# Softmax denominators as 128 queries by 8 in an attention block: one small inversion, turned together with the next head's maxima

## The chip, the cores and the metric

The kernel runs on one core of a Trainium2 chip. It is one launch, written out instruction by instruction for each engine: TensorE multiplies matrices, VectorE, ScalarE and GpSimd work on elements, and SyncE issues the transfers. The engines run side by side and are held together by semaphores alone. The metric is the device time of the launch in microseconds (us).

## What is computed

A transformer block on x of shape 2 x 1024 x 128: a modulated attention layer with 16 query heads of 64 (4 key heads), rotary positions and an ALiBi bias, then two layers of local attention and gated MLP. The change touches the first attention alone, whose core is

```
attn = einsum('bhqd,bhkd->bhqk', q, k) / sqrt(64)
attn = attn + slopes[None, :, None, None] * rel[None, None, :, :]
attn = softmax(attn, axis=-1)
out  = einsum('bhqk,bhkd->bhqd', attn, v)
```

Two batches of 16 heads make 32 heads of 1024 queries by 1024 keys. Softmax needs of each query its maximum over the keys, ahead of the exponential, and the sum of the exponentials, its denominator, by which the output is divided.

## The kernel before

The heads run one after another. Each is cut into eight steps k of 128. Two different tilings are in use. The *maxima* of head i+2 are taken with 128 queries on the partitions and 1024 keys along the row (`max_step`: a product on TensorE into banks 4 and 5, L836, then one VectorE instruction that adds the ALiBi row and keeps the negated maximum, L765). They end as a tile M of 128 queries by 8 steps. The *scores* proper have 128 keys on the partitions and 1024 queries along the row (`qk_step`, L862, into banks 0 and 1 or 2 and 3, by turns; the exponential on ScalarE, L738; the product with the values, `pv_step`, L872, into bank 6 or 7). So the maxima are needed as a row over the queries: TensorE turns M (`turn_m`, L842), ScalarE copies it out (`take_m`, L721), and SyncE moves it into QM (`load_m`, L639), from where it enters the score product of the next head.

The denominators of head i-1 are made in head i. GpSimd and VectorE add up the eight exponentials into `sum_p` (128 keys by 1024 queries). TensorE sums over the partitions with a stationary block of ones, 32 wide, four times 256 queries, so that the result stands on four groups of partitions as 256 queries a row (`denominators`, L881, into bank 0). ScalarE copies it out (`take_denominators`, L715), VectorE inverts it in two halves of 128 columns, each spread over all 128 partitions (`invert`, L782). SyncE stores the 1024 inverses to memory and loads them back, broadcast over the partitions (`spread_inverse`, L645 and L649), and VectorE multiplies the finished output by them (`divide`, L790), which frees the bank of head i-1 for head i+1.

The order is written out by hand. TensorE runs, for each pair of steps k, k+1: two score steps, the maxima of step k of head i+2, two value steps (k-1 and k), and the maxima of step k+1. Behind the value steps of the second pair stand the small products: the denominators of head i-1 and the turn of head i+1. The score step k = 4 waits for the two copies on ScalarE, since bank 0 holds the denominators and bank 1 the turned maxima. The first value step of head i waits until head i-2 is divided. VectorE runs the maxima k = 0 to 7, with a sum ahead of k = 0, the inversions behind k = 2 and 3, another sum behind k = 5 and the two divisions behind k = 6. SyncE runs in a head: the loads for later heads, `load_m`, then `spread_inverse`.

Of the kernel before, what the change touches and what calls it, by code (L numbers as in the profile page):

```python
# [13 lines left out]
P = 128  # L14
B, N, D = 2, 1024, 128
TB = N // P
# [75 lines left out]
def adaln_block(nc, x, wq, wk, wv, wo, f_wqkv, f_qs, f_ks, f_wo, f_lg, f_lb, f_w1, f_b1, f_w2, f_b2,  # L92
# [7 lines left out]
    with ExitStack() as whole:  # L100
# [478 lines left out]
        DQ = N // 4  # L579
        with ExitStack() as ph:  # L580
# [3 lines left out]
            M = sb("M", [P, 2, TB])  # L584
            mrow = sb("mrow", [TB, 2, P], F32R)
# [4 lines left out]
            den_sb = XF[:, TB + 2:TB + 2 + DQ // P, :].rearrange("p t d -> p (t d)")  # L590
            den_inv = XF[:, TB:TB + DQ // P, :].rearrange("p t d -> p (t d)")
# [10 lines left out]
            m_turned = sem("m_turned")  # L602
            mrow_done = sem("mrow_done")
# [6 lines left out]
            den_taken = sem("den_taken")  # L610
# [14 lines left out]
            def m_bank(i):  # L625
                return 1 if i > 0 else 7
# [4 lines left out]
            with nc.Block() as block:  # L631
                @block.sync
                def _(sp):
                    def load_m(i, s):

                        sp.wait_ge(qm_filled, 3)
                        need(sp, mrow_done, i + 1)
                        for ch in range(2):
                            sp.dma_start(QM[HD * ch:HD * ch + 1, s, :].bitcast(F32).rearrange("p (t c) -> p t c", c=P),  # L639
                                         mrow[TB // 2 * ch:TB // 2 * (ch + 1), s, :].bitcast(F32)).then_inc(ld_m[s], 16)  # L640

                    def spread_inverse(i, s):

                        need(sp, inv_done, 2 * (i + 1))
                        sp.dma_start(inv_d[s].rearrange("(c n) -> c n", n=DQ), den_inv[0:P:32, :]).then_inc(inv_out, 16)  # L645
# [56 lines left out]
                def _(act):  # L702
# [9 lines left out]
                    def take_denominators(i):  # L712
                        need(act, den_mm, i + 1)
                        need(act, inv_done, 2 * i)
                        act.activation(den_sb[:, :], banks(den_bank(i))[:, 0:DQ], ACT.Copy)\  # L715
                            .then_inc(den_taken, 1)

                    def take_m(i, s):
                        need(act, m_turned, i + 1)
                        need(act, ld_m[s], 32 * (i // 2))  # L720
                        act.activation(mrow[:, s, :], banks(m_bank(i))[0:TB, 0:P], ACT.Copy).then_inc(mrow_done, 1)  # L721

                    def head(i):
                        for k in range(TB):
                            if k == 4 and i > 0:
                                take_denominators(i - 1)
                            if k == 4 and i + 1 < HEADS:
                                take_m(i + 1, (i + 1) % 2)
# [21 lines left out]
                    take_m(0, 0)  # L750
# [809 lines left out]
```

## Time and profile before

| | |
|---|---|
| time, median of 3 runs | 1317.8 us (1313.16 to 1318.82) |
| the profiled execution | 1316.46 us, of which the span of the trace is 1314.7 |
| busy share of the span | TensorE 85%, VectorE 80%, GpSimd 65%, ScalarE 56% |
| exponentials, L738 | 256 of 1112 ns, 274.8 us |
| maxima on VectorE, L765 | 256 of 1209 ns, 309.4 us |
| inversions, L782 | 64 of 948 ns, 60.4 us, and 64.1 us of idle time ahead of them |
| copy of the denominators, L715 | 32 of 383 ns, 12.3 us |

In the rows, PE is TensorE's products and PEld its loads of the stationary operand, DVE is VectorE, ACT ScalarE, POOL GpSimd, and SPq the issuing of transfers by SyncE. A product of 32-bit numbers appears as two records, each with its own load: the four products of the denominators are eight. Matrix products overlap, so that starts are more telling than durations. "M" and "mrow" are the maxima, "XF" is the memory in which denominators and inverses lie, "xpos_sb" that of the sums.

### The profile page before, as it was taken

How to read it: one execution, taken by the hardware profiler on the slowest of the kernel's cores; microseconds unless marked ns; L12 is line 12 of the kernel's file. 1: busy time of each engine (PE TensorE's matmuls, PEld its weight loads, DVE VectorE, ACT ScalarE, POOL GpSimd, SP SyncE). 2: the span in 40 equal slices, each digit the busy share in tenths (PEclk: the TensorE clock that was granted, in tenths of full speed). 3: DMA queues.
4: the chain of work that ended last, by engine and by line, in shares of the span. 5: the costliest groups of instructions: out<-in, count | busy, mean ns of one | idle time of the engine just before them, and what ended most of it. 6: DMA issues, size and time to landing. Idle time of an engine off the chain costs nothing. (4 is left out here: it accounts for less than half of the span.)

```text
span 1314.7 us, 23737 instructions
## 1 busy us (share of the span) xinstructions
PE 1115.1 (85%) x8256; PEld 692.6 (53%) x8256; DVE 1049.2 (80%) x2026; ACT 735.6 (56%) x1512; POOL 849.0 (65%) x488
## 2 busy tenths in 40 slices
PE   5776579999999999999999999467777896778788
PEld 3554535544455454555445548234555684455578
DVE  6898577777777777777777746599999589999957
ACT  3666625555555555555555551257676755777664
POOL 4556216566566666656656664698789249999916
PEclk9888769999999999999999999789898997999899
DMA  7567932142413314241331001000111100111111
GB/s 230 136 173 198 283 80 57 42 97 65 105 42 86 76 42 97 65 105 38 83 83 52 23 17 56 34 17 19 27 28 28 31 3 8 27 28 29 30 31 33
DMA packets 95237, 88.91 MB, mean 68 GB/s; under 512 B 22884, under 2 KB 74768, under 8 KB 95120
## 3 DMA queue, kind: packets, MB, share of 16 engines
q1 hardware_dynamic: 95120, 87.41, 26.2%
q8 instruction: 66, 1.08, 0.3%
q14 instruction: 51, 0.42, 0.1%
HBM read 53.57 MB, written 24.25 MB: 59 GB/s over the span
## 5 line engine op out<-in xcount | busy, mean ns | idle before, releaser
L738 ACT ACTIVATE E<-psum,keybias_sb 128x1024 f32<-128x1024 f32 x256 | 274.8, 1112 | 249.1 <-PE psum L862 235.9
L765 DVE CUSTOM_DVE_ANT_0 junk<-psum,alibi 128x1024 bf16<-128x1024 f32 x256 | 309.4, 1209 | 93.0 <-PE psum L836 80.2
L684 POOL TENSOR_TENSOR xpos_sb<-xpos_sb,E 128x1024 f32<-128x1024 f32 x96 | 231.2, 2408 | 130.7 <-ACT E L738 126.2
L872 PE MATMUL psum<-E,V 128*64 128x512 f32 x1024 | 248.0, 605 | 0.0
L836 PE MATMUL psum<-KH,QH 64*128 64x512 f32 x512 | 124.7, 481 | 20.9 <-DVE M L765 16.7
L688 POOL TENSOR_TENSOR xpos_sb<-xpos_sb 128x1024 f32<-128x1024 f32 x32 | 76.1, 2377 | 90.7 <-DVE xpos_sb L775 90.7
L1195 ACT ACTIVATE E_att<-S_att,nmax_att 128x128 f32<-128x128 f32 x256 | 99.0, 389 | 43.7 <-DVE nmax_att L1229 43.6
L1142 POOL TENSOR_TENSOR rinv_att<-ss_up_att,minus_half 128x16 f32<-128x16 f32 x32 | 120.8, 3775 | 2.7
L872 PEld LDWEIGHTS psum<-E,V 128*64 128x64 f32 x1024 | 62.1, 136 | 112.7 <-issue 105.7
L836 PEld LDWEIGHTS psum<-KH,QH 64*128 64x128 f32 x512 | 50.6, 191 | 124.1 <-DVE M L765 92.6
L782 DVE RECIPROCAL XF<-XF 128x128 f32<-128x128 f32 x64 | 60.4, 948 | 64.1 <-ACT XF L715 64.1
L862 PE MATMUL psum<-QH,KH 64*128 64x512 f32 x512 | 106.4, 406 | 3.4 <-ACT XF L715 1.0
L862 PE MATMUL psum<-QL,KH 64*128 64x512 f32 x512 | 103.4, 392 | 0.0
L862 PE MATMUL psum<-QH,KL 64*128 64x512 f32 x512 | 103.1, 391 | 0.0
L862 PE MATMUL psum<-QM,one_rows 64*128 64x512 f32 x512 | 103.0, 390 | 0.0
L1132 POOL TENSOR_TENSOR t_att<-raw_att,xpos_sb 128x1024 f32<-128x1024 f32 x32 | 100.5, 3142 | 0.0
L1323 PE MATMUL psum<-kT_att,qT_att 64*64 64x128 f32 x1024 | 42.4, 310 | 66.3 <-DVE nmax_att L1229 66.1
L684 POOL TENSOR_TENSOR xpos_sb<-E 128x1024 f32<-128x1024 f32 x32 | 76.4, 2388 | 30.0 <-ACT E L738 24.8
L1248 DVE TENSOR_TENSOR qk_att<-qk_att,rinv_att 128x1024 f32<-128x1024 f32 x32 | 90.3, 2823 | 5.8 <-POOL rinv_att L1142 4.7
L1323 PEld LDWEIGHTS psum<-kT_att,qT_att 64*64 64x64 f32 x1024 | 33.9, 152 | 88.6 <-issue 88.0
L1127 POOL TENSOR_TENSOR sq_att<-raw_att 128x1024 f32<-128x1024 f32 x32 | 66.6, 2083 | 14.1 <-ACT raw_att L1202 14.1
L1313 PE MATMUL psum<-fw_qkv,hT_att 128*128 128x512 f32 x128 | 66.1, 642 | 2.1 <-ACT raw_att L1202 2.1
(145 smaller groups left out, 2399.9 us busy)
## 6 DMA issues: line engine op xcount, KB each, us to landing
qa_scratch<-tT SPq DMA_DIRECT2D x32, 512.0 KB, 4.1
QH<-qa_scratch SPq DMA_DIRECT2D x64, 256.0 KB, 4.2
QL<-qa_scratch SPq DMA_DIRECT2D x64, 128.0 KB, 4.2
XF<-inverse_scratch SPq DMA_DIRECT2D x64, 128.0 KB, 2.9
vp_att<-v_att SPq DMA_DIRECT2D x64, 128.0 KB, 2.3
k_scratch<-tT SPq DMA_DIRECT2D x16, 256.0 KB, 4.6
KH<-k_scratch SPq DMA_DIRECT2D x16, 256.0 KB, 3.9
KL<-k_scratch SPq DMA_DIRECT2D x16, 256.0 KB, 5.1
```

Source lines behind the costliest of these rows:

```text
L684: pool.tensor_tensor(sum_p[:, s, :], first, E[:, k % 4, :], ALU.add)\
L688: pool.tensor_tensor(sum_p[:, s, :], sum_p[:, s, :], sum_d[:, s, :], ALU.add)\
L738: act.activation(E[:, k % 4, :], scores(k % 2), ACT.Exp, bias=kb).then_inc(exp_done, 1)
L765: dve.tensor_tensor_reduce(junk[:, :], banks(max_bank(i, k), 2), alibi[:, s, :], -1.0, BIG, ALU.add, ALU.min, M[:, s, k:k + 1]).then_inc(m ...
L836: last = pe.matmul(banks(max_bank(i, k) + ch), QH[rows, s, k * P:(k + 1) * P], KH[rows, g, ch * 512:(ch + 1) * 512], start=True, stop=True)
L862: last = pe.matmul(scores(k % 2)[:, ch * 512:(ch + 1) * 512], key[rows], query[rows, a:a + 512], start=(n == 0), stop=(n == len(terms) - 1))
L872: last = pe.matmul(banks(6 + i % 2)[HD * ch:HD * ch + HD, :], V[:, g, k, :], E[:, k % 4, ch * 512:(ch + 1) * 512], start=(k == 0), stop=(k ...
L1132: pool.tensor_tensor(t2[:, s].rearrange("p (q h) d -> p q h d", q=2), raw[:, s].rearrange("p (q h) d -> p q h d", q=2), sin, ALU.mult)\
L1142: pool.tensor_tensor(rinv[:, s, :], ss_up[:, s, :], minus_half[:, 0:NH], ALU.pow)\
L1195: act.activation(E[:, s, h, :], S[:, s, h, :], ACT.Exp, bias=nmax[:, s, h:h + 1], scale=-1.0, accum_out=den[:, s, h:h + 1]).then_inc(exp_d ...
L1248: dve.tensor_tensor(qk[:, s], qk[:, s], rinv[:, s, :][:, :, None].to_broadcast([P, NH, HD]), ALU.mult).then_inc(qk_done, 1)
L1323: last = pe.matmul(banks(5 + h % 2)[WIN * w:WIN * w + WIN, (h // 2) * P:(h // 2 + 1) * P], qT[a:a + HD, s, h // 2, WIN * w:WIN * w + WIN], ...
```

## The change

The denominators are made with the sum stationary and one column of ones moving: eight products, each of which gives 128 queries on the partitions in one column, 128 by 8 in all. VectorE inverts them straight from bank 0 in one instruction, into a tile `stats` beside the maxima. Where the maxima of head i+1 were turned alone (8 columns), one turn now takes them and the inverses of head i-1 (16 columns); one copy on ScalarE takes both out, and SyncE stores the inverses from eight rows of 128. The copy of the denominators and its semaphore are gone.

The order changes with it. The denominators stay where they were on TensorE. The turn moves from behind them to behind the value steps of the third pair (k = 4); the copy from ScalarE's step 4 to step 6; the inversion stands behind the maxima of k = 3, and the divisions move from behind the maxima of k = 6 to behind those of k = 7. The score step k = 4 waits for the inversion, and k = 6 for the copy. At the end of the stage the last turn stands behind the fourth tile of the output projection.

```diff
 def spread_inverse(i, s):
-    need(sp, inv_done, 2 * (i + 1))
-    sp.dma_start(inv_d[s].rearrange("(c n) -> c n", n=DQ), den_inv[0:P:32, :]).then_inc(inv_out, 16)
+    need(sp, turned_done, i + 3)
+    sp.dma_start(inv_d[s].rearrange("(t c) -> t c", c=P), turned[TB:2 * TB, s, :]).then_inc(inv_out, 16)
...
-def take_denominators(i):
-    need(act, den_mm, i + 1)
-    need(act, inv_done, 2 * i)
-    act.activation(den_sb[:, :], banks(den_bank(i))[:, 0:DQ], ACT.Copy).then_inc(den_taken, 1)
-def take_m(i, s):
-    need(act, m_turned, i + 1)
-    need(act, ld_m[s], 32 * (i // 2))
-    act.activation(mrow[:, s, :], banks(m_bank(i))[0:TB, 0:P], ACT.Copy).then_inc(mrow_done, 1)
+def take_turned(i, s):
+    need(act, stats_turned, i + 1)
+    need(act, ld_m[s], 32 * min(i // 2, HEADS // 2))
+    need(act, inv_out, 16 * (i - 3))
+    rows = TB if i < 2 else 2 * TB
+    act.activation(turned[0:rows, s, :], banks(turn_bank(i))[0:rows, 0:P], ACT.Copy).then_inc(turned_done, 1)
...
-            if k == 4 and i > 0:
-                take_denominators(i - 1)
-            if k == 4 and i + 1 < HEADS:
-                take_m(i + 1, (i + 1) % 2)
+            if k == 6:
+                take_turned(i + 1, (i + 1) % 2)
...
-def invert(i, half):
-    need(dve, den_taken, i + 1)
-    need(dve, inv_out, 16 * i)
-    part = slice(half * DQ // 2, (half + 1) * DQ // 2)
-    dve.reciprocal(den_inv[:, part], den_sb[:, part]).then_inc(inv_done, 1)
+def invert(i, s):
+    need(dve, den_mm, i + 1)
+    need(dve, stats_turned, i + 1)
+    dve.reciprocal(stats[:, s, 1, :], banks(den_bank(i))[:, 0:TB]).then_inc(inv_done, 1)
...
-            if k in (2, 3) and i > 0:
-                invert(i - 1, k - 2)
+            if k == 3 and i > 0:
+                invert(i - 1, (i - 1) % 2)
...
-            if k == 6 and i > 0:
+            if k == 7 and i > 0:
                 for ch in range(2):
                     divide(i - 1, ch)
...
 def denominators(i, s):
-    for c in range(4):
-        last = pe.matmul(banks(den_bank(i))[32 * c:32 * c + 32, 0:DQ], ones[:, :],
-                         sum_p[:, s, c * DQ:(c + 1) * DQ], start=True, stop=True)
+    for c in range(TB):
+        last = pe.matmul(banks(den_bank(i))[:, c:c + 1], sum_p[:, s, c * P:(c + 1) * P], ones[:, 0:1],
+                         start=True, stop=True)
...
 def qk_step(i, k):
         if k == 4:
-            need(pe, den_taken, i)
-            need(pe, mrow_done, min(i + 2, HEADS))
+            need(pe, inv_done, i)
+        if k == 6:
+            need(pe, turned_done, i + 2)
```

TensorE in the middle of a head, before: behind two value steps (E, V) the denominators (`ones_m`), the turn of the maxima M, the maxima of step 3, and the score step 4 with its waits.

```order
L872 MATMUL psum<-E,V 64x512
L881 MATMUL psum<-xpos_sb,ones_m 32x256 [waits sum_p_done,filled]
L881 MATMUL psum<-xpos_sb,ones_m 32x256 x3
L842 MATMUL psum<-ident,M 8x128 [waits max_done]
L836 MATMUL psum<-KH,QH 128x512 [waits max_done]
L836 MATMUL psum<-KH,QH 128x512
L862 MATMUL psum<-QH,KH 128x512 [waits exp_done,mrow_done,den_taken]
```

The same place now, and the end of the next round, where the turn of `stats` stands.

```order
L873 MATMUL psum<-ones_m,xpos_sb 128x1 [waits sum_p_done,filled]
L873 MATMUL psum<-ones_m,xpos_sb 128x1 x7
L824 MATMUL psum<-KH,QH 128x512 [waits max_done]
L824 MATMUL psum<-KH,QH 128x512
L854 MATMUL psum<-QH,KH 128x512 [waits exp_done,inv_done]
...
L864 MATMUL psum<-E,V 64x512
L832 MATMUL psum<-ident,stats 16x128 [waits inv_done,max_done]
L824 MATMUL psum<-KH,QH 128x512 [waits max_done]
L824 MATMUL psum<-KH,QH 128x512
L854 MATMUL psum<-QH,KH 128x512 [waits exp_done,turned_done]
```

The turn has left its place between denominators and maxima and comes a round later; the score step 4 waits for VectorE instead of ScalarE, and the score step 6 has a new wait.

VectorE, before, from the maxima of step 5 on (`junk,M`) to the first maxima of the next head.

```order
L775 TENSOR_TENSOR xpos_sb<-E 128x1024 [waits sum_p_done,sum_d_done,exp_done]
L765 ISA junk,M<-psum,alibi 128x1024 [waits max_done,max_mm]
L765 ISA M 128x1
L790 TENSOR_TENSOR OT<-psum,XF 64x512 [waits pv_done,inv_in] x2
L765 ISA junk,M<-psum,alibi 128x1024 [waits max_done,max_mm]
L765 ISA M 128x1
L775 TENSOR_TENSOR xpos_sb<-xpos_sb,E 128x1024 [waits sum_d_done,exp_done]
L765 ISA junk,M<-psum,alibi 128x1024 [waits m_turned,max_done,alibi_done,max_mm]
```

The same stretch now.

```order
L766 TENSOR_TENSOR xpos_sb<-E 128x1024 [waits sum_p_done,sum_d_done,exp_done]
L756 ISA junk,stats<-psum,alibi 128x1024 [waits max_done,max_mm]
L756 ISA stats 128x1
L756 ISA junk,stats<-psum,alibi 128x1024 [waits max_done,max_mm]
L756 ISA stats 128x1
L779 TENSOR_TENSOR OT<-psum,XF 64x512 [waits pv_done,inv_in] x2
L766 TENSOR_TENSOR xpos_sb<-xpos_sb,E 128x1024 [waits sum_d_done,exp_done]
L756 ISA junk,stats<-psum,alibi 128x1024 [waits stats_turned,max_done,alibi_done,max_mm]
```

The two divisions (OT), which wait for the loaded inverses, have moved behind the last maxima; behind them now stand the sum and the first maxima of the next head.

## Rows read from the trace of the kernel before

**Rows 1.** The page's first line: the span.

```profile
span 1314.7 us, 23737 instructions
```

**Rows 2.** Busy time by stretch: length, busy us (records) by engine, clock, transfers' share, GB/s.

```profile
240.00:780.00 540.00, 528.71 (x3398) 270.42 (x3394) 411.71 (x607) 283.79 (x308) 337.63 (x142) 1.00 0.27 68
```

**Rows 3.** Timeline, TensorE's loads: start, us, instruction; denominators of first and 29th head.

```profile
212.08 0.16 PEld L881 LDWEIGHTS psum<-xpos_sb,ones_m 128*32 128x32 f32 x8 [0.81 <-issue]
...
750.80 0.16 PEld L881 LDWEIGHTS psum<-xpos_sb,ones_m 128*32 128x32 f32 x8 [0.81 <-issue]
```

**Rows 4.** Timeline, TensorE's loads in one regular head.

```profile
289.11 0.16 PEld L881 LDWEIGHTS psum<-xpos_sb,ones_m 128*32 128x32 f32 x8 [0.81 <-issue]
...
289.68 0.08 PEld L842 LDWEIGHTS psum<-ident,M 128*8 128x8 f32 x1 [0.41 <-issue]
...
289.88 0.19 PEld L836 LDWEIGHTS psum<-KH,QH 64*128 64x128 f32 x2
...
290.42 0.21 PEld L862 LDWEIGHTS psum<-QH,KH 64*128 64x128 f32 x2 [0.35 <-ACT XF L715]
...
294.62 0.19 PEld L836 LDWEIGHTS psum<-KH,QH 64*128 64x128 f32 x2 [0.81 <-DVE M L765]
...
298.98 0.19 PEld L836 LDWEIGHTS psum<-KH,QH 64*128 64x128 f32 x2 [0.81 <-DVE M L765]
...
308.06 0.16 PEld L881 LDWEIGHTS psum<-xpos_sb,ones_m 128*32 128x32 f32 x8 [0.81 <-issue]
```

**Rows 5.** Timeline of the same head, ScalarE and VectorE.

```profile
290.10 0.25 ACT L721 ACTIVATE mrow<-psum 8x128 fp32r<-8x128 f32 x1
...
293.67 1.15 ACT L708 ACTIVATE alibi<-far_sb,slope_sb 128x1024 f32<-128x1024 f32 x1
...
295.16 1.23 DVE L765 CUSTOM_DVE_ANT_0 junk<-psum,alibi 128x1024 bf16<-128x1024 f32 x1 [0.94 <-PE psum L836]
...
301.17 1.22 DVE L775 TENSOR_TENSOR xpos_sb<-xpos_sb,E 128x1024 f32<-128x1024 f32 x1
302.31 1.22 DVE L765 CUSTOM_DVE_ANT_0 junk<-psum,alibi 128x1024 bf16<-128x1024 f32 x1
```

**Rows 6.** Timeline, transfers and divisions: the regular head, then a fourth one.

```profile
290.42 1.29 SPq L639 DMA_DIRECT2D QM<-mrow  x2
293.17 0.51 SPq L645 DMA_DIRECT2D inverse_scratch<-XF  x1
294.83 1.14 SPq L649 DMA_DIRECT2D XF<-inverse_scratch  x2
...
298.59 1.40 DVE L790 TENSOR_TENSOR OT<-psum,XF 64x512 f32<-64x512 f32 x2
...
504.64 0.52 SPq L645 DMA_DIRECT2D inverse_scratch<-XF  x1
507.60 1.14 SPq L649 DMA_DIRECT2D XF<-inverse_scratch  x2
...
511.58 1.41 DVE L790 TENSOR_TENSOR OT<-psum,XF 64x512 f32<-64x512 f32 x2 [1.43 <-DMA XF<-inverse_scratch]
```

**Rows 7.** Timeline, three runs of loads elsewhere in the kernel.

```profile
4.69 2.63 PEld L461 LDWEIGHTS psum<-silu,wmod_sb 128*128 128x128 f32 x12 [4.69 <-DMA wmod_sb<-in_L_wmod_dram]
...
795.58 3.65 PEld L543 LDWEIGHTS psum<-wo_sb,OT 128*128 128x128 f32 x32 [0.81 <-issue]
...
891.18 0.89 PEld L1323 LDWEIGHTS psum<-kT_att,qT_att 64*64 64x64 f32 x32 [2.78 <-issue]
```

**Rows 8.** Instructions by line: busy us, mean ns, idle before; a small reciprocal.

```profile
L1267 DVE RECIPROCAL den_inv_att<-den_att 128x8 f32<-128x8 f32 x32 | 6.1, 192 | 8.9 <-ACT E_att L1195 8.9
```

**Rows 9.** Busy time by stretch, columns as in rows 2.

```profile
881.00:884.30 3.30, 0.88 (x3) 0.06 (x1) 3.27 (x2) 2.01 (x4) 2.85 (x2) 1.00 0.05 12
884.40:887.60 3.20, 2.61 (x10) 2.32 (x11) 3.17 (x5) 1.45 (x3) 1.37 (x2) 0.50 0.29 64
...
512.60:514.40 1.80, 0.22 (x2) 0.03 (x1) 1.77 (x4) 1.46 (x2) 0.00 (x0) 1.00 0.66 150
```

## What the change will do to the time

> **What bounds the kernel now.** I read the profile in this order: the page for the span, the busy time by stretch, the timeline of one head of the attention stage, engine by engine, and then single rows as prices. The profiled execution has a span of 1314.7 us [rows 1] and a device time of 1316.46 us, 1.76 us more; the sum below is made against 1316.5. The median of the three timed runs, 1317.8, is 1.3 above it. The change lies wholly in the attention stage of 32 heads. There TensorE is busy 528.7 of 540 us at the high clock, VectorE 411.7, ScalarE 283.8, GpSimd 337.6 [rows 2]. So TensorE's own order is the bound, and a microsecond taken from VectorE or ScalarE is worth nothing unless TensorE waits for it.
>
> The denominators of one head are issued once per head, so their rows are a ruler: from the first at 212.08 to the one at 750.80 lie 28 heads, 19.24 us each [rows 3]. A regular head runs from 289.11 to 308.06, 18.95 us [rows 4]. It has four rounds of the same work (odd maxima, two score steps, even maxima, two value steps) with a small insert. The unhindered round is 294.62 to 298.98, 4.36 us. The first, 289.88 to 294.62, takes 4.74, since the fifth score step waits for ScalarE's copies until 290.42; from that step to the round's end are 4.20. Denominators and turn together take 0.77 (289.11 to 289.88). The last two rounds take 9.08, which is 0.36 over twice 4.36. So four rounds are 17.44, the insert 0.77, and only about 0.75 is waiting. The reciprocals that the change shrinks cost almost nothing there.
>
> **Denominators.** Before: four products, in the trace eight records of 32 stationary and 256 moving columns, 0.57 us (289.11 to 289.68 [rows 4]). After: eight products with 128 stationary columns and one moving, so 16 loads of 128 columns with nothing long to hide behind. The nearest row is the output projection, 32 pairs of load and product of 128 columns in 3.65 us, 0.114 each [rows 7], which gives 16 x 0.114 = 1.83. Lower bound: 32 pairs of 64x64 in 0.89 us, 0.028 each, 0.45 in all; upper: 12 pairs of 128 stationary and 2 moving columns at the kernel's start, 2.63 us, 0.219 each, 3.5 in all [rows 7]. I take 1.83, since the loads there have the same width and clock, and call it D.
> The Trainium skill ("TensorE: Matmul & The Clock Gate", LDWEIGHTS) says that a load costs by its columns, whatever the rows; the row agrees. The same page's table of issue gaps (Back-to-back issue gap) gives about 60 cycles at 2.4 GHz for any product of up to 64 moving columns; by that, 16 would be 0.4 us and the sum some 40 us lower.
>
> **The wait at the fifth score step.** It now waits for the inversion, because the denominators lie in its bank. On VectorE the inversion stands behind the maxima of step 3, and those stand behind their product on TensorE, issued after the denominators. Walk, from the start of the denominators: product at D, VectorE starts 0.54 later (294.62 to 295.16), the maxima take 1.23, an inversion of 128x8 takes 0.19 [rows 4, 5, 8], and the signal 0.07 (ScalarE done at 290.35, TensorE on at 290.42 [rows 4, 5]). The step starts at D + 2.03. Before it started 0.54 behind that product. The queue behind it is the whole of TensorE: score steps, maxima, value steps.
>
> **The turn, moved behind the value steps.** It starts at D + 2.03 + 4.20 = D + 6.23. Before, its copy on ScalarE was done 0.67 after it (289.68 to 290.35) and the next consumer ran at 0.74. ScalarE is free by then: its two exponentials and the ALiBi row end at 294.82, 4.4 behind the fifth score step [rows 5], here at D + 6.4. So the seventh score step, which waits for the copy, starts at D + 6.97, and the third round begins at D + 6.97 + 4.20 = D + 11.17. ScalarE's other copy goes; it was hidden behind TensorE's maxima.
>
> **The inverse's way through memory.** Here is the main loss. SyncE first issues the two transfers of the next maxima, 1.29, at D + 6.97, then the store at D + 8.3. From store to first load: 1.66 (293.17 to 294.83); from first load to the division that waited for it: 3.98 (507.60 to 511.58) [rows 6]. The divisions can start at D + 13.9; the two take 1.41, done at D + 15.35. Before, the store was issued 4.06 behind the denominators (293.17), and the division found its data there with no wait at 298.59 in a regular head [rows 6].
> The divisions now stand behind the last maxima, which frees the first maxima of the next head from them; but the first value step of the next head needs their bank. It would run at D + 11.17 + 4.36 - 0.93 = D + 14.6 and runs at D + 15.4: 0.8 waited. More weighs what is queued behind them on VectorE: the sum (1.14) and the maxima of step 0 (1.22) [rows 5], and TensorE's maxima of step 1 need that bank pair: 15.35 + 1.14 + 1.22 + 0.07 = D + 17.8, where the round would have ended at D + 15.5. The fourth round adds 4.36: the next denominators start at D + 22.16. They close the loop, since it leads from denominators to denominators: its length is the new period, 1.83 + 22.16 = 24.0 us.
>
> **Cover.** VectorE loses two long reciprocals a head and gains one of 0.19; worth nothing, as VectorE is idle a quarter of the stage [rows 2]. GpSimd's last sum starts once VectorE's sum is done (D + 16.5), and the next denominators, which need it, come 5.6 later. The maxima's transfers land some 2 us behind D + 8.3, needed at D + 11.3: hidden, with 1 us to spare. One thing is better: in each fourth head the store took 2.96 until the load (504.64 to 507.60 [rows 6]), beside the key and value loads; the later store is clear of those. The average of 19.24 contains that loss, so it is counted.
>
> **Sum.** 28 heads x (24.0 - 19.24) = 133. The two heads without maxima lose less, about 2.5 each as an estimate from the same walk, since nothing stands ahead of the inversion and behind the division: 5. At the end the last turn waits for two projection tiles (3.65, [rows 7]) instead of ScalarE: 1 to 2. Together 139.5: 1456 us with the clock untouched.
>
> **The clock.** In [rows 9] the granted clock is 1.00, that is 2.4 GHz, in 881.0 to 884.3, where TensorE was busy 0.88 of 3.3 us, and 0.50, or 1.2 GHz, in the 3.2 us behind. In 512.6 to 514.4, with 0.22 busy of 1.8 between full stretches, it was not lost. The new head has, from the denominators to the fifth score step, D + 2.03 = 3.9 us with 0.34 us of streaming products in it; whether 16 loads with one column each keep the clock up, no row shows. A stretch at the low level as long as that row's costs half of it, 1.65 us, and here wholly on the loop. I take it for a third of the heads, 9 x 1.65 = 14: **forecast 1470 us**. If the one-column products count as work, it is 1456; if not, two thirds of the heads or more, 1487.
> The Trainium skill (same page, Part 1: The HAM clock gate) says that activity releases the throttle and idling brings it back; by that the second case is open, and its price is the one just worked out from rows.
>
> **Rivals.** (1) The loop as walked, clock kept or lost in part: 1445 to 1495, chance 0.70. (2) The clock is lost in most heads and loads run at 0.219: D = 3.5 adds 1.7 x 28 = 47 to 1475: 1495 to 1530, chance 0.13. (3) One-column products are cheap, D = 0.45: 1.38 x 28 = 39 off, 1417 with the clock kept and 1431 with it lost as above: 1410 to 1435, chance 0.13. (4) Not slower: the loop through the inverse does not close, because the inverse lands before the next head's first value step and the inversion slips in before the fifth score step; then TensorE's own work stands, 17.44 + 0.20 + D. That is 19.5 with D = 1.83, 7 us slower in all; with D below 1.6 it is equal, with D = 0.45, 18.1, 32 us faster, 1284. For it speaks that TensorE is 98% busy; against it that both waits are in the order and the walk has them 1.5 and 3.1 us late. That the change would not do what it says is out: the order shows the small inversion and the joint turn where the text puts them. Chance 0.04.
>
> **How the numbers follow.** The range, 1425 to 1525, reaches from part of (3) to nearly all of (2) and leaves some 0.15 out. About 0.5% is what a measurement of this kernel can tell from no change. Faster by more 0.02, within 0.01, slower 0.97.
>
> **What would show each step.** The period of the denominators near 24 us instead of 19.2; their duration near 1.8; a TensorE wait of about 1.5 us for the inversion ahead of the fifth score step; the store about D + 8.3 behind them; waits for the division ahead of a value step and for the maxima behind it; granted clock below 1.00 in some heads. The prediction is wrong if the fifth step does not wait, or if the divisions start earlier than 12 us behind the denominators.

## The result, and the profile after

The changed kernel takes 1507.6 us (median of four runs, 1500.21 to 1515.13) against 1317.4 us for the kernel before on the same chip: the ratio is 1.145 (95% interval 1.141 to 1.148). It is 14.5% slower. The forecast was 1470 us with a range of 1425 to 1525: the sign and the range hold, the point is 38 us too low. The profiled execution took 1500.21 us.

The page of the changed kernel, first line and busy time by engine:

```profile
span 1498.3 us, 24196 instructions
...
PE 1222.4 (82%) x8514; PEld 774.4 (52%) x8514; DVE 1009.2 (67%) x1994; ACT 730.6 (49%) x1482; POOL 845.2 (56%) x488
```

The span grew by 183.6 us [rows 1]. VectorE was busy 80% of the shorter span and is now busy 67% of the longer one: the long reciprocals are gone, and nothing was gained by it. The busy time by stretch (columns as in rows 2) of the middle of the attention stage:

```profile
240.00:750.00 510.00, 448.06 (x2604) 245.93 (x2606) 274.44 (x424) 202.23 (x203) 238.52 (x101) 0.91 0.22 55
```

TensorE was busy 98% of such a stretch [rows 2]; it is now busy 88%, and the granted clock has fallen from 1.00 to 0.91. Both parts matter below.

The ruler of [rows 3], the first denominators and those 28 heads later (timeline, TensorE's loads), and the transfer with which the next block begins:

```profile
212.64 1.86 PEld L873 LDWEIGHTS psum<-ones_m,xpos_sb 128*128 128x128 f32 x16 [0.81 <-issue]
...
918.14 1.86 PEld L873 LDWEIGHTS psum<-ones_m,xpos_sb 128*128 128x128 f32 x16 [0.81 <-issue]
...
993.56 0.37 SPq L929 DMA_DIRECT2D mask_sb<-in_mask_dram  x1
```

The 28 heads take 705.50 us, 25.20 each, where they took 19.24: 166.8 us of the 183.6. They are not alike. Three of them, each from its denominators to the next (busy time by stretch, columns as in rows 2):

```profile
489.31:515.52 26.21, 23.20 (x132) 12.48 (x130) 13.64 (x21) 10.00 (x10) 11.88 (x6) 0.87 0.29 69
515.52:540.32 24.80, 21.86 (x131) 12.03 (x129) 13.63 (x21) 10.01 (x10) 11.82 (x6) 0.93 0.16 43
565.50:588.98 23.48, 20.35 (x131) 11.03 (x130) 13.63 (x21) 9.89 (x10) 11.84 (x6) 1.00 0.30 75
```

Ten heads are like the first, with the clock at 0.87 and 26.0 us on average; 17 are like the second, with 0.93 and 24.8; only the third keeps 1.00. The clock falls in all the others, and in the ten its time at the low level is about twice as long. The end of the stage is the other piece. From the 29th denominators to the first transfer of the next block (mask_sb) it was 811.26 - 750.80 = 60.5 us (its row before is below), and it is 993.56 - 918.14 = 75.4: 14.9 more. What is left, 1.9, lies ahead of the first denominators and behind the stage.

```profile
811.26 0.34 SPq L938 DMA_DIRECT2D mask_sb<-in_mask_dram  x1
```

One head, first the way through memory (timeline; denominators of this head at 489.31, those of the next at 515.52):

```profile
500.14 0.09 PEld L832 LDWEIGHTS psum<-ident,stats 128*16 128x16 f32 x1 [0.87 <-issue]
...
500.45 0.27 ACT L713 ACTIVATE turned<-psum 16x128 f32<-16x128 f32 x1 [1.34 <-PE psum L832]
500.77 0.18 PEld L854 LDWEIGHTS psum<-QH,KH 64*128 64x128 f32 x2 [0.24 <-ACT turned L713]
...
500.79 1.29 SPq L635 DMA_DIRECT2D QM<-turned  x2
...
502.13 0.46 SPq L641 DMA_DIRECT2D inverse_scratch<-turned  x1
...
503.53 1.15 SPq L645 DMA_DIRECT2D XF<-inverse_scratch  x2
...
507.15 1.41 DVE L779 TENSOR_TENSOR OT<-psum,XF 64x512 f32<-64x512 f32 x2 [0.44 <-DMA XF<-inverse_scratch]
...
508.59 1.23 DVE L766 TENSOR_TENSOR xpos_sb<-xpos_sb,E 128x1024 f32<-128x1024 f32 x1
...
508.71 1.08 PE L864 MATMUL psum<-E,V 128*64 128x512 f32 x4 [0.20 <-DVE OT L779]
509.85 1.23 DVE L756 CUSTOM_DVE_ANT_0 junk<-psum,alibi 128x1024 bf16<-128x1024 f32 x1
...
511.14 0.49 PE L824 MATMUL psum<-KH,QH 64*128 64x512 f32 x2 [1.35 <-DVE stats L756]
```

It reads as one chain: turn (500.14), copy, transfer of the maxima, store (502.13), load (503.53), divisions (507.15), sum (508.59), maxima of step 0 (509.85), and TensorE's maxima of step 1, which wait 1.35 for them (511.14). In [rows 6] the divisions of a regular head waited for nothing. The transfer itself is late by only 0.44 here; store_first below asks what that is worth.

Then the next head's denominators and what stands behind them:

```profile
515.52 1.86 PEld L873 LDWEIGHTS psum<-ones_m,xpos_sb 128*128 128x128 f32 x16 [0.81 <-issue]
...
517.39 0.19 PEld L824 LDWEIGHTS psum<-KH,QH 64*128 64x128 f32 x2
...
517.94 1.23 DVE L756 CUSTOM_DVE_ANT_0 junk<-psum,alibi 128x1024 bf16<-128x1024 f32 x1 [2.94 <-PE psum L824]
...
519.09 0.20 DVE L771 RECIPROCAL stats<-psum 128x8 f32<-128x8 f32 x1
...
519.35 0.50 PE L854 MATMUL psum<-QH,KH 64*128 64x512 f32 x2 [1.45 <-DVE stats L771]
```

The inversion takes 0.20 us but stands behind maxima of 1.23, and TensorE waits 1.45 for it. What that does to the clock shows in the busy time of the same place: from the denominators to the fifth score step, and the 3.2 us behind it.

```profile
515.50:519.30 3.80, 2.40 (x20) 2.05 (x18) 1.35 (x3) 0.00 (x0) 1.82 (x1) 1.00 0.00 0
519.70:522.90 3.20, 3.20 (x18) 2.24 (x14) 0.00 (x0) 1.21 (x2) 0.60 (x1) 0.52 0.00 0
```

TensorE runs the waiting stretch at the high level and is then granted 0.52, practically 1.2 GHz, in full work. The Trainium skill ("TensorE: Matmul & The Clock Gate", Part 1: The HAM clock gate) says that idling brings the throttle back; this row agrees. The same wait of 1.45 also stands in the head from 565.50, which keeps its clock: the wait does not lower it every time.

The waits of the changed kernel between 240 and 910 us (engine, what waited, for what: total us, times, longest):

```profile
PE psum L854 <- DVE stats L771: 39.1, 27, 1.5
PE psum L824 <- DVE stats L756: 35.1, 26, 1.4
...
DVE OT L779 <- DMA XF<-inverse_scratch: 12.9, 27, 1.9
...
PE psum L864 <- DVE OT L779: 5.0, 11, 1.6
```

Two waits of about 1.4 us stand in practically every head (27 and 26 times), one for the inversion and one for the maxima behind the divisions. They don't do the same to the clock: in all 27 heads that lose it, the busy times by stretch show the low level beginning 2.5 to 5 us behind the denominators, in or right behind the first of these waits, and never behind the second, which follows work of full length. The value step waited for the divisions in 11 heads only, 5.0 us in all. No load of TensorE waited longer than 0.81 in [rows 4].

### The profile page after: what moved, and what is told of

It reads as the page before. It is cut to its first block and busy times, and to the rows that moved or that the text cites. A ratio compares the mean times of both kernels' runs of the same rounds, so it can differ in the third digit from the quotient of the medians.

```text
span 1498.3 us, 24196 instructions
## 1 busy us (share of the span) xinstructions
PE 1222.4 (82%) x8514; PEld 774.4 (52%) x8514; DVE 1009.2 (67%) x1994; ACT 730.6 (49%) x1482; POOL 845.2 (56%) x488
## 5 line engine op out<-in xcount | busy, mean ns | idle before, releaser
L756 DVE CUSTOM_DVE_ANT_0 junk<-psum,alibi 128x1024 bf16<-128x1024 f32 x256 | 313.4, 1224 | 339.4 <-PE psum L824 326.5
L729 ACT ACTIVATE E<-psum,keybias_sb 128x1024 f32<-128x1024 f32 x256 | 278.0, 1113 | 458.6 <-PE psum L854 451.2
L680 POOL TENSOR_TENSOR xpos_sb<-xpos_sb,E 128x1024 f32<-128x1024 f32 x96 | 227.0, 2365 | 270.0 <-ACT E L729 265.6
L864 PE MATMUL psum<-E,V 128*64 128x512 f32 x1024 | 263.6, 626 | 7.1 <-DVE OT L779 6.2
L854 PE MATMUL psum<-QH,KH 64*128 64x512 f32 x512 | 121.2, 469 | 44.0 <-DVE stats L771 42.6
L854 PE MATMUL psum<-QH,KL 64*128 64x512 f32 x512 | 114.0, 441 | 0.0
L854 PE MATMUL psum<-QL,KH 64*128 64x512 f32 x512 | 113.9, 441 | 0.0
L854 PE MATMUL psum<-QM,one_rows 64*128 64x512 f32 x512 | 113.1, 437 | 0.0
L680 POOL TENSOR_TENSOR xpos_sb<-E 128x1024 f32<-128x1024 f32 x32 | 76.5, 2391 | 30.0 <-ACT E L729 24.8
L854 PEld LDWEIGHTS psum<-QH,KH 64*128 64x128 f32 x512 | 54.5, 209 | 70.9 <-DVE stats L771 51.9
L1314 PEld LDWEIGHTS psum<-kT_att,qT_att 64*64 64x64 f32 x1024 | 35.1, 158 | 85.9 <-issue 85.3
L873 PEld LDWEIGHTS psum<-ones_m,xpos_sb 128*128 128x128 f32 x512 | 59.6, 191 | 26.5 <-issue 26.5
```

The costliest lines, as they stand in the source:

```text
L680: pool.tensor_tensor(sum_p[:, s, :], first, E[:, k % 4, :], ALU.add)\
L729: act.activation(E[:, k % 4, :], scores(k % 2), ACT.Exp, bias=kb).then_inc(exp_done, 1)
L756: dve.tensor_tensor_reduce(junk[:, :], banks(max_bank(i, k), 2), alibi[:, s, :], -1.0, BIG, ALU.add, ALU.min, stats[:, s, 0, k:k + 1]).the ...
L854: last = pe.matmul(scores(k % 2)[:, ch * 512:(ch + 1) * 512], key[rows], query[rows, a:a + 512], start=(n == 0), stop=(n == len(terms) - 1))
L864: last = pe.matmul(banks(6 + i % 2)[HD * ch:HD * ch + HD, :], V[:, g, k, :], E[:, k % 4, ch * 512:(ch + 1) * 512], start=(k == 0), stop=(k ...
L1314: last = pe.matmul(banks(5 + h % 2)[WIN * w:WIN * w + WIN, (h // 2) * P:(h // 2 + 1) * P], qT[a:a + HD, s, h // 2, WIN * w:WIN * w + WIN], ...
```

## The experiments

The theory is that of the prediction: a loop from denominators to denominators through the inversion, the turn and the memory sets the period, and the granted clock takes a part on top. The rivals are that the one-column products set the time by themselves, and that the clock sets it. All ratios are against the kernel before, run beside on the same chip. "In a head" is the average over the same 28 heads; "the clock" is the granted clock in 240 to 750 us, where it was 0.91 in the changed kernel.

| | us | ratio (95%) | in a head | clock |
|---|---|---|---|---|
| the change | 1507.6 | 1.145 (1.141 to 1.148) | 25.20 | 0.91 |
| fill_wait | 1460.4 | 1.109 (1.105 to 1.113) | 23.82 | 0.99 |
| inverse_first | 1427.9 | 1.084 (1.079 to 1.088) | 22.69 | 0.96 |
| store_first | 1487.7 | 1.129 (1.126 to 1.131) | 24.70 | 0.91 |
| den_twice | 1588.5 | 1.206 (1.201 to 1.211) | 27.78 | 0.86 |
| turn_early | 1420.8 | 1.079 (1.077 to 1.080) | 22.64 | 0.95 |
| turn_early_den_early | 1401.0 | 1.064 (1.062 to 1.066) | 21.95 | 0.97 |
| order_restored | 1358.2 | 1.031 (1.028 to 1.033) | 20.45 | 0.99 |
| before_loads | 1386.6 | 1.052 (1.051 to 1.054) | 21.32 | 0.98 |
| before_div_late | 1339.4 | 1.017 (1.015 to 1.018) | 19.99 | 1.00 |
| before_den_early | 1311.8 | 0.996 (0.994 to 0.997) | 19.00 | 1.00 |
| before_den_early_split | 1315.4 | 0.998 (0.997 to 0.999) | 19.20 | 1.00 |

### The clock alone: fill_wait

The changed kernel, with work that is thrown away put into the wait for the inversion:

```diff
+def fill(i):
+    g, s = (i // GROUP) % 2, i % 4
+    need(pe, exp_done, TB * i + 3)
+    for n in range(6):
+        pe.matmul(banks(1), KH[:, g, 0:P], QH[:, s, 0:512], start=True, stop=True)
...
             if i + 2 < HEADS:
                 max_step(i + 2, k + 1)
+            if k == 2 and 0 < i < HEADS - 2:
+                fill(i)
```

> The changed kernel, and in each head, behind the maxima of step 3 on TensorE, six products of 512 columns into bank 1, whose result nobody reads: about 1.3 us of streaming work in the 1.5 us in which TensorE waits for the inversion. Nothing is taken from the order. If the fall of the clock behind this quiet stretch makes the difference between the walk (1456 us) and the measured 1507.6, the clock stays at 1.00 in most heads and the time is 1455 to 1470, in spite of more work. If the loop itself is longer than walked and the clock is a bystander, the time stays at 1500 to 1515, or rises by what the products delay.

It took 1460.4 us (1458.33 to 1466.31), 47 less than the changed kernel with more work in it. The timeline of TensorE's loads, and the busy time by stretch:

```profile
569.20 1.86 PEld L873 LDWEIGHTS psum<-ones_m,xpos_sb 128*128 128x128 f32 x16 [0.81 <-issue]
...
571.50 1.24 PEld L881 LDWEIGHTS psum<-QH,KH 128*128 128x128 f32 x6 [0.24 <-issue]
...
573.10 0.18 PEld L854 LDWEIGHTS psum<-QH,KH 64*128 64x128 f32 x2 [0.36 <-DVE stats L771]
```

```profile
240.00:750.00 510.00, 473.62 (x2890) 261.68 (x2890) 290.95 (x448) 213.41 (x216) 253.22 (x107) 0.99 0.24 57
```

The fifth score step still starts 3.9 us behind the denominators, so the wait is the same wait; only the engine is no longer quiet in it, and the clock stays at 0.99. So the lowered clock was worth at least 47 us by the medians (1.4 in each of the 28 heads, 25.20 - 23.82, by the two profiles). It is a little more, since 5 of the 28 heads still lose the clock here and take 25.1 on average; the other 23 take 23.53. With 23.53 in all of them, an estimate from these two numbers, the loop alone gives some 1452, against 1456 in the walk.

### The wait at the fifth score step: inverse_first

The changed kernel, with the inversion ahead of the maxima of step 3 on VectorE:

```diff
-            if i + 2 < HEADS:
-                max_step(i + 2, i % 2, k)
             if k == 3 and i > 0:
                 invert(i - 1, (i - 1) % 2)
+            if i + 2 < HEADS:
+                max_step(i + 2, i % 2, k)
```

> The changed kernel with the inversion ahead of the maxima of step 3 on VectorE instead of behind them. If the wait at the fifth score step is the one walked (product of step 3, its maxima, then the inversion), it shrinks from 1.5 us to under 0.4 and each of 28 heads is some 1.4 us shorter: 1467 us with the clock falling as now, and down to 1415 if the clock then stays up, since the quiet stretch ends 1.4 us sooner. If the divisions set the period whatever comes before them, the time stays near 1505.

1427.9 us (1422.65 to 1435.54): 80 less. The timeline of one head:

```profile
507.69 1.86 PEld L873 LDWEIGHTS psum<-ones_m,xpos_sb 128*128 128x128 f32 x16 [0.81 <-issue]
...
509.68 0.21 DVE L771 RECIPROCAL stats<-psum 128x8 f32<-128x8 f32 x1 [2.50 <-PE psum L873]
...
509.94 0.18 PEld L854 LDWEIGHTS psum<-QH,KH 64*128 64x128 f32 x2 [0.18 <-DVE stats L771]
```

The inversion starts 1.99 behind the start of the denominators, and the fifth score step at 2.25 instead of 3.83: 1.6 shorter. The clock now stays in half of the heads; these take 21.7 on average instead of 23.5, the others 23 and more; over the stretch it reads 0.96. One swap of two instructions takes back 80 of the 190 us, by the shorter loop and by a clock that falls less often. Of the 2.5 us that a head gains on average, 1.8 are the loop (23.53, the heads of fill_wait that keep the clock, to 21.74) and 0.7 the clock.

### The place of the store: store_first

The changed kernel, with the store of the inverses issued ahead of the two transfers of the maxima:

```diff
 def load_m(i, s):
...
     need(sp, turned_done, i + 1)
+    if i > 1:
+        store_inverse(i - 2, i % 2)
     for ch in range(2):
```

> The changed kernel, in which SyncE stores the inverses ahead of the two transfers of the next maxima instead of behind them. If the loop runs through the inverse's way through memory, the divisions come about 1.3 us earlier and so do the value step and the maxima behind them: 28 x 1.3 = 36 less, 1471 us. If TensorE's own work or the wait for the inversion alone sets the period, and the division would be hidden by either, nothing changes: 1505.

1487.7 us (1486.66 to 1488.17): 20 less, not 36. The timeline of VectorE ahead of the divisions, and the wait for the load over 240 to 900 us:

```profile
501.69 0.08 DVE L762 DVE_READ_ACCUMULATOR2_ANT stats<- 128x1 f32 x1
501.80 1.41 DVE L785 TENSOR_TENSOR OT<-psum,XF 64x512 f32<-64x512 f32 x2
```

```profile
DVE OT L785 <- DMA XF<-inverse_scratch: 1.2, 2, 1.0
```

The wait for the transfer is gone (12.9 us before, 1.2 now), and the divisions start right behind the read of the last maxima. So the transfer was late by only some 0.5 us in a head; take it away, and the next thing that was late is the place of the divisions behind the maxima of step 7. TensorE's wait for the maxima behind the divisions stays (33.3 us in 26 heads; it was 35.1). The expectation had left that out.

### The price of the one-column products: den_twice and before_loads

den_twice makes the denominators of the changed kernel twice over; before_loads adds the same eight products to the kernel before, into a free part of the bank, and uses them for nothing.

```diff
-for c in range(TB):
+for c in 2 * list(range(TB)):
     last = pe.matmul(banks(den_bank(i))[:, c:c + 1], sum_p[:, s, c * P:(c + 1) * P], ones[:, 0:1],
```

> The changed kernel with the eight products of the denominators issued twice over, with the same result. If the 1.86 us of the one-column products lie wholly on the loop, each of 31 heads is 1.86 longer: 1565 us, and up to 20 more if the longer quiet stretch costs the clock more often. If half of them were hidden behind something, 1535 or less.

```diff
 need(pe, sum_p_done, NP * (i + 1))
+for c in range(TB):
+    pe.matmul(banks(den_bank(i))[:, DQ + c:DQ + c + 1], sum_p[:, s, c * P:(c + 1) * P], ones[:, 0:1],
+              start=True, stop=True)
 for c in range(4):
```

> The kernel before, with the eight one-column products issued ahead of its own four and never read: the products of the change without its order. If their 1.86 us lie wholly on TensorE's path, 31 x 1.86 = 58 more, 1375 us; if they also cost the clock by themselves, without any wait behind them, 1385 to 1410. If they were hidden in waits, under 1340.

den_twice: 1588.5 us (1583.58 to 1597.15), 81 more than the changed kernel. Its 32 loads in one head:

```profile
520.10 4.24 PEld L873 LDWEIGHTS psum<-ones_m,xpos_sb 128*128 128x128 f32 x32 [0.81 <-issue]
```

31 more sets at 1.87 are 58 us. A head takes 2.58 more; in the one shown the 32 loads take 4.24, more than twice 1.86, and the clock falls to 0.86 over 240 to 750 us. The 81 lie just above the top of what was expected (78).

before_loads: 1386.6 us (1385.69 to 1389.35), 68.9 more than the kernel before. Its ruler:

```profile
469.83 1.86 PEld L881 LDWEIGHTS psum<-ones_m,xpos_sb 128*128 128x128 f32 x16 [0.81 <-issue]
...
492.15 1.86 PEld L881 LDWEIGHTS psum<-ones_m,xpos_sb 128*128 128x128 f32 x16 [0.81 <-issue]
...
513.10 1.86 PEld L881 LDWEIGHTS psum<-ones_m,xpos_sb 128*128 128x128 f32 x16 [0.81 <-issue]
```

Again 58 us are the products. Most heads take 20.8 to 21.0; seven of the 28 lose the clock and take some 1.4 more (469.83 to 492.15, 22.32), which is nearly all of the other 11 us, and over the stretch the clock reads 0.98. So with only the short wait of the kernel before behind them (0.35 at the fifth score step), the one-column products cost the clock in a quarter of the heads; in the changed kernel, with 1.45 us of waiting behind them, it is lost in 27 of 28. There they take the place of 0.57 us a head, so that 1.87 - 0.57 by 31, or 40 us of the 190, are theirs: the rival that they set the time by themselves is out.

### The divisions: before_div_late

The kernel before, with only the divisions moved behind the maxima of step 7:

```diff
-            if k == 6 and i > 0:
+            if k == 7 and i > 0:
                 for ch in range(2):
```

> The kernel before with nothing but its divisions moved behind the maxima of step 7, as the change has them. By the walk the wait for the maxima of step 7 (0.36 a head) goes, and one of 1.2 comes ahead of the maxima of step 1, since the divisions and the sum now stand ahead of the maxima of step 0: 0.8 a head, 1340 us. In the fourth heads, where the transfer is late, it gains instead. If the move costs nothing, as the change's writer may have held, 1310 to 1320.

1339.4 us (1338.94 to 1339.88), 22 more. The divisions need no wait for their data, and TensorE waits for the first maxima of the next head, as in the changed kernel:

```profile
505.68 1.40 DVE L790 TENSOR_TENSOR OT<-psum,XF 64x512 f32<-64x512 f32 x2
...
509.66 0.50 PE L836 MATMUL psum<-KH,QH 64*128 64x512 f32 x2 [1.20 <-DVE M L765]
```

So moving them costs 0.75 us a head with the clock at 1.00, although VectorE has a quarter of its time free.

### Taking the order back: turn_early, turn_early_den_early, order_restored

Three kernels with the changed layout and one inversion, and ever more of the old order. turn_early: the inversion first as in inverse_first, and the turn behind the maxima of step 3, with its copy at ScalarE's step 4 and the wait for the copy at the fifth score step (only the turn is shown).

```diff
             if i + 2 < HEADS:
                 max_step(i + 2, k + 1)
+            if k == 2:
+                turn_stats(i + 1, (i + 1) % 2)
...
```

> The changed kernel with the order near that of before: the inversion ahead of the maxima of step 3 on VectorE, the turn right behind the denominators on TensorE, ScalarE's copy ahead of its step 4; the divisions stay behind the maxima of step 7. The wait for the inversion is then some 0.3 us and the inverses are stored 4.2 us behind the denominators, so that only two things of the change stay on TensorE's path: 1.3 us more of loads and the divisions ahead of the next head's sum and maxima, some 1.3 us. Walked: 21.4 us a head instead of 25.2, 1380 us with the clock kept, 1400 if it still falls in part. If it was not the order that cost the time, the result stays above 1430, as with the inversion alone moved.

turn_early_den_early: in addition the denominators ahead of the value steps of the second pair, and the turn behind these.

```diff
-            pv_step(i, k)
             if k == 2 and i > 0:
+                need(pe, exp_done, TB * i + 3)
                 denominators(i - 1, (i - 1) % 2)
+            pv_step(i, k)
+            if k == 2:
                 turn_stats(i + 1, (i + 1) % 2)
```

> The same with the denominators between the two value steps of the round instead of behind them, so that a value step of 0.9 us covers the inversion. Walked: 0.6 us a head less than with the turn early alone, 1362 us with the clock kept. If the clock falls because of the one-column products themselves, the value step between them and the next wait gives back more.

order_restored: in addition the divisions back behind the maxima of step 6.

```diff
-            if k == 7 and i > 0:
+            if k == 6 and i > 0:
                 for ch in range(2):
```

> The changed kernel with its stationary sums and its small inversion, but with the order of before or better: inversion ahead of the maxima of step 3, turn ahead of them on TensorE, denominators between the two value steps, divisions behind the maxima of step 6. What is left of the change is then its 1.3 us more of loads a head: 19.24 + 1.3 - 0.4 for the wait that the early denominators remove is 20.1 us a head, 1342 us, and up to 1375 with what the clock still loses. If the small inversion is worth something in itself, under 1318.

turn_early took 1420.8 us (1419.41 to 1423.1), only 7 less than inverse_first and 20 over the top of what was expected. The turn comes a round earlier, yet a head with the clock kept takes 21.6, as in inverse_first (21.7). It is the same as in store_first: with the inverse early, the divisions stand behind the maxima of step 7, which don't come earlier. And 18 of the 28 heads lose the clock and take 23.2:

```profile
503.28 0.50 PE L824 MATMUL psum<-KH,QH 64*128 64x512 f32 x2 [1.21 <-DVE stats L756]
```

```profile
240.00:750.00 510.00, 472.89 (x2918) 271.79 (x2920) 309.28 (x476) 226.67 (x227) 267.83 (x112) 0.95 0.26 64
```

TensorE still waits 1.21 for the first maxima of the next head. turn_early_den_early took 1401.0 us (1399.71 to 1406.21): 20 less, 0.69 in a head. The 0.6 that was expected of the shorter wait did not come: heads with the clock kept take 21.3 instead of 21.6. The rest is the clock, which falls in 12 heads instead of 18. The absolute time that was expected was 39 too low, for the same two reasons.

order_restored took 1358.2 us (1355.32 to 1362.3): 43 less, 1.5 in a head, by moving the divisions alone. Heads with the clock kept go from 21.3 to 20.4, and only 2 of the 28 lose it. The divisions still run without a wait, and the clock is nearly back:

```profile
509.17 1.40 DVE L779 TENSOR_TENSOR OT<-psum,XF 64x512 f32<-64x512 f32 x2
```

```profile
240.00:750.00 510.00, 507.22 (x3219) 281.34 (x3217) 337.04 (x524) 246.69 (x250) 297.66 (x125) 0.99 0.28 68
```

What is left of the change in this kernel, layout and small inversion, costs 40 us against the kernel before. But the early denominators are a gain that the change doesn't have, so the fair partner is before_den_early below, with 19.00 in a head: 20.45 is 1.45 more, of which 1.86 - 0.57 = 1.29 are the longer denominators and 0.09 the two heads that lose the clock. Nothing is left for the smaller inversion to have gained.

### A better kernel: before_den_early and its split form

If the order is what counts, the kernel before may gain from it. before_den_early moves its small products (denominators and turn) ahead of the value steps of the second pair, so that ScalarE's copies are done under them.

```diff
-            pv_step(i, k)
             if k == 2:
+                need(pe, exp_done, TB * i + 3)
                 small_products(i)
+            pv_step(i, k)
```

> The kernel before with denominators and turn between the two value steps of the round instead of behind them. ScalarE's two copies then run beside a value step, and the wait of 0.38 us at the fifth score step goes: 28 x 0.38 = 11 less, 1307 us. If that wait was hidden by another one that is next, 1317.

before_den_early_split also puts one of the two divisions behind the maxima of step 6 and the other behind those of step 7.

```diff
-            if k == 6 and i > 0:
-                for ch in range(2):
-                    divide(i - 1, ch)
+            if k >= 6 and i > 0:
+                divide(i - 1, k - 6)
```

> The same, and the two divisions of a head apart: one behind the maxima of step 6, one behind those of step 7. The maxima of step 7 come 0.7 us sooner, and the wait of 0.36 us ahead of the next head's first maxima on TensorE goes, while the maxima of step 0 stand where they stood: 1297 us, 18.5 us a head. In the other case, that the division or the sum behind it delays step 0, 1307 or more.

before_den_early took 1311.8 us (median of seven, 1308.97 to 1314.74): 0.996 of the kernel before (0.994 to 0.997), a regular head 18.73 to 18.87. It is the fastest of all, but it gains 6.6 us (0.24 in a head) where 11 were expected, and 0.43% is less than the 0.5% that the prediction named as what a measurement of this kernel can tell. The split form took 1315.4 us (median of twelve, 1312.99 to 1317.11), a miss against 1297, and the other case of its expectation: the late loads of each fourth head no longer show, but every head is 19.1 instead of 18.8.

```profile
511.23 0.69 DVE L790 TENSOR_TENSOR OT<-psum,XF 64x512 f32<-64x512 f32 x1
...
513.34 0.69 DVE L790 TENSOR_TENSOR OT<-psum,XF 64x512 f32<-64x512 f32 x1
...
516.61 0.50 PE L835 MATMUL psum<-KH,QH 64*128 64x512 f32 x2 [0.62 <-DVE M L765]
```

The second division goes behind maxima that themselves wait for TensorE, and pushes the sum and the next head's maxima back: TensorE waits 0.62 at 516.61. As in store_first and turn_early, a VectorE instruction put behind a maximum is tied to TensorE's order, however idle VectorE is.

## Why the prediction was right, and what was mis-sized

By its time alone, 1507.6 us lies outside the 1445 to 1495 of the prediction's own case (1) and in the 1495 to 1530 of rival (2). The mechanism is that of (1) with the clock lost far more often; so the number stands in the range, but not in its favoured part.

**Denominators.** 1.83 was predicted from the output projection [rows 7]; measured are 16 loads in 1.86 and the next load at 1.87 (517.39 - 515.52). The cheap rival with 0.45, and the dear one with 3.5, are both out. The sum of the dear one also starts from 1475, which the text works out nowhere; from its own 1487 it would have been 1534.

**The wait at the fifth score step.** The product's start, VectorE 0.55 behind it, 1.15 until the inversion starts, 0.20, and the score step at D + 1.95 (519.34), against D + 2.03. Right, and it is in every head (27 of 27).

**The way through memory.** In the head shown, the turn takes 0.63 until the seventh score step (walk 0.74), the store is issued 1.36 behind it (walk 1.3), the load 1.40 behind the store (walk 1.66), the divisions 3.62 behind the load (walk 3.98). The last two steps were each some 0.3 too long, taken from the nearest rows, and the head with the clock kept takes 23.48 against 24.0; its divisions start at D + 13.3 (walk D + 13.9) and TensorE's maxima behind them at D + 17.25 (walk D + 17.8). But the sentence "Here is the main loss" is wrong. By store_first the transfer is late by 0.5 us a head, 20 us in all. Take it away and the divisions still stand behind the maxima of step 7, ahead of the next head's sum and maxima, and TensorE's wait stays; before_div_late shows the same loss with the inverses in time. The walk's times hold because the transfer does end last, but by half a microsecond only, and the text did not look at what ends just ahead of it. From the divisions on, the walk had 1.14 for the sum and 1.22 for the maxima, and 0.07: with the 1.41 of the divisions 3.84 until TensorE's maxima; measured 3.99 (507.15 to 511.14). The value step waited 0.20 (508.71) where 0.8 was foretold, and the maxima behind it 1.35. Rival (4) is out, since both of its waits are there, and the order through the divisions closes the loop with or without the transfer. fill_wait gives 1460 for it, some 1452 without its five slow heads, where the walk had 1456.

**The clock: the term that was mis-sized.** What failed is the sentence "I take it for a third of the heads, 9 x 1.65 = 14" (9 by 1.65 is 14.9). The clock fell in 27 of 28 heads, and fill_wait puts its price at 47 us. The price of one fall was sized about right: heads at 0.93 take 24.8, which is 1.3 over the 23.5 of those that keep the clock, against 1.65. But in ten heads, at 0.87, the time at the low level is about twice as long and costs 2.5. So the count was too small by a factor of three, and the longer stay was not foreseen; why it comes in these ten heads, no run shows. The text itself had a larger count, "two thirds of the heads or more, 1487", as a case. Rival (2) foretold the clock's fall in most heads, but bound it to loads of 0.219, and these stayed at 0.117. What the count rested on was [rows 9]: 0.88 busy in 3.3 us lost the clock, 0.22 in 1.8 did not. The 3.8 us here lie nearer the first in length. That the page of busy times counts them as 2.40 busy did not save the clock; of that, 1.86 are one-column products.

**The end of the stage.** Predicted were 5 for the last two heads and 1 to 2 for the end; measured 14.9. The rows of the end:

```profile
973.57 1.41 DVE L779 TENSOR_TENSOR OT<-psum,XF 64x512 f32<-64x512 f32 x2 [4.42 <-DMA XF<-inverse_scratch]
...
978.77 1.86 PEld L873 LDWEIGHTS psum<-ones_m,xpos_sb 128*128 128x128 f32 x16 [1.33 <-issue]
...
985.75 0.09 PEld L832 LDWEIGHTS psum<-ident,stats 128*16 128x16 f32 x1
...
987.78 1.08 SPq L645 DMA_DIRECT2D XF<-inverse_scratch  x2
```

By the starts of the denominators, 12.0 of the 14.9 lie in the last three heads (22.99, 19.53 and 18.11, where they took 17.94, 17.00 and 13.66), and 2.9 behind the last denominators. In the last head the divisions wait 4.42 us for the memory, with no maxima to hide it, and the last turn comes 6.98 behind the last denominators. The walk had taken off the waits that the missing maxima cause and forgot that the way through memory stays as long. No experiment took this piece apart; that is a reading of these rows.

**The sum again.** The loop with the clock kept is 28 heads by 4.29 (23.53 against 19.24), or 120, predicted 133. The clock is 47 in these heads (28 by 1.67), predicted 14 over the whole stage. The end is 15, predicted 6.5. With the 1.9 left over these are the 183.6 of the span, against 153.5. The misses have both signs: 13 too many in the loop hide part of the 33 and 8 too few in the clock and at the end.

## What to carry to other kernels

Before an operation is made smaller, look whether anything waits for it: here the reciprocals lay beside TensorE's work, and the smaller one was put where TensorE waits. Walk the loop from one of its turns to the next through every engine and queue, and where a walk takes one wait away, name the next instruction that is late before counting the gain; store_first and turn_early missed by that, and the split form fell to its worse case. A wait of one or two microseconds on TensorE is also a risk to its clock: count it in full unless a row of the same length and with the same kind of work shows otherwise.

## What was not expected of the hardware

- A stretch of 1.86 us of one-column products and 1.45 us of waiting lowered the granted clock in 27 of 28 heads (0.91 over the stage, 0.52 in the work behind), though the trace counts TensorE busy in the first. Six products of 512 columns in the same wait kept it at 0.99, and the kernel with more work was 47 us faster. A wait of 1.35 us behind full work, later in the same heads, never lowered it.
- The one-column products without the long wait lowered it in 7 of 28 heads (22.3 to 22.5 us among heads of 20.9; 0.98 over the stage).
- A product of one column costs what its stationary operand costs to load: 0.117 us each, 16 in 1.86. Its single column saves nothing against the 0.57 us of the wide form with 32 stationary columns.
